# Causal attention with 16 heads of 64: query, key and value projections in three rounded terms instead of whole fp32

## What is computed

```python
def _L3_xattn_ref(q, k, v, Wq, Wk, Wv, Wo):
    query = jnp.einsum('bse,hed->bhsd', q, Wq)
    key_p = jnp.einsum('bse,hed->bhsd', k, Wk)
    value = jnp.einsum('bse,hed->bhsd', v, Wv)
    scores = jnp.einsum('bhqd,bhkd->bhqk', query, key_p) / jnp.sqrt(64)
    causal = jnp.tril(jnp.ones((S, S), dtype=scores.dtype))
    scores = scores + (1.0 - causal) * NEG
    alphas = jax.nn.softmax(scores, axis=-1)
    attention = jnp.einsum('bhqk,bhkd->bhqd', alphas, value)
    attention = attention.reshape(B, S, NUM_HEADS * VALUE_DIM)
    return jnp.einsum('bsf,fe->bse', attention, Wo)
...
x = x + _L3_xattn_ref(_layernorm(x), ctx_1024, ctx_1024, Wq, Wk, Wv, Wo)
```

## Time and profile before

| | us |
|---|---|
| median of 3 runs | 1894.47 |
| lowest, highest | 1890.64, 1900.73 |
| the profiled execution | 1900.78 |
| its span in the trace | 1899.0 |
| TensorE busy | 1516.8 (80%) |
| VectorE busy | 963.4 (51%) |
| stage of the change, from its first transfer to the last score step | about 1371 to 1815 |

### The profile page before, as it was taken

How to read it: one execution, slowest core, us unless ns; L and a number is a source line. 1 busy time by engine, 2 the same in 40 slices (tenths; PEclk the granted TensorE clock), 3 DMA queues, 4 the chain that set the end, 5 groups by cost and what they waited for, 6 DMA issues and landing times. The chain is left out here.

```text
span 1899.0 us, 34141 instructions
## 1 busy us (share of the span) xinstructions
PE 1516.8 (80%) x12506; PEld 1188.3 (63%) x12506; DVE 963.4 (51%) x1962; ACT 688.9 (36%) x1527; POOL 493.3 (26%) x833
## 2 busy tenths in 40 slices
PE   3898684865878842999458999997699999999876
PEld 2565473754656542888336666664378888888765
DVE  2676352446645541111456677776326655555652
ACT  1565333321544410111126656665342323332121
POOL 2210027016534303000411355540032323332110
PEclk8899778886889855999769999998799999999986
DMA  5331192446644226886466645452120000000001
GB/s 137 80 77 39 50 351 80 144 139 155 158 109 107 56 83 244 312 313 221 133 155 135 143 104 115 113 114 47 37 73 7 7 7 2 7 7 2 2 7 45
DMA packets 89772, 195.51 MB, mean 103 GB/s; under 512 B 14000, under 2 KB 62512, under 8 KB 81040
## 3 DMA queue, kind: packets, MB, share of 16 engines
q1 hardware_dynamic: 76688, 172.97, 32.2%
q0 software_dynamic: 4608, 12.59, 2.1%
q10 hardware_dynamic: 8320, 7.87, 1.2%
HBM read 136.37 MB, written 57.02 MB: 102 GB/s over the span
## 5 line engine op out<-in xcount | busy, mean ns | idle before, releaser
L987 DVE TENSOR_REDUCE a_sb_mx<-a_mx 128x4 f32<-128x1024 f32 x192 | 234.7, 1222 | 116.6 <-PE a_mx L809 114.0
L730 ACT ACTIVATE a_sb_probs<-a_ex 128x512 f32<-128x512 f32 x384 | 208.8, 598 | 154.7 <-PE a_ex L830 154.3
L1349 DVE RECIPROCAL a_sb_rden<-a_ot 128x256 f32<-128x256 f32 x64 | 112.0, 1750 | 99.4 <-PE a_ot L1233 99.4
L830 PE MATMUL a_ex<-a_sb_QP,a_sb_KP 49*128 49x256 f32 x768 | 99.5, 336 | 32.6 <-ACT a_sb_probs L730 25.9
L266 POOL DMA_INDIRECT a_sb_landing<-f_y_slots,g_pos x48 | 46.6, 970 | 277.6 <-POOLq L143 264.2
L830 PEld LDWEIGHTS a_ex<-a_sb_QP,a_sb_KP 49*128 49x128 f32 x768 | 61.3, 192 | 87.6 <-issue 57.2
L809 PE MATMUL a_mx<-a_sb_KP,a_sb_QP 48*128 48x256 f32 x768 | 89.5, 310 | 33.1 <-DVE a_sb_mx L987 21.2
L843 PE MATMUL a_ot<-a_sb_probs,a_sb_v 128*32 128x256 f32 x1536 | 109.2, 404 | 2.1 <-ACT a_sb_probs L730 2.1
L809 PEld LDWEIGHTS a_mx<-a_sb_KP,a_sb_QP 48*128 48x128 f32 x768 | 62.9, 197 | 45.6 <-DVE a_sb_mx L987 25.5
L1135 POOL TENSOR_TENSOR a_sb_q_lo<-a_sb_whole,a_sb_q_hi 128x512 fp32r<-128x512 f32 x32 | 40.6, 1269 | 172.6 <-ACT a_sb_q_hi L1164 172.6
L2670 PE MATMUL f_hb<-f_sb_xsT,f_sb_wb 128*128 128x128 f32 x640 | 75.2, 279 | 10.9 <-ACT f_sb_xsT L2623 10.9
(11 more groups left out here) (414 smaller groups left out, 3554.2 us busy)
## 6 DMA issues: line engine op xcount, KB each, us to landing
f_sb_wb<-f_w SPq DMA_DIRECT2D x20, 2052.0 KB, 10.2
a_q_moved<-a_sb_qs SPq DMA_DIRECT2D x24, 512.0 KB, 6.1
a_sb_QP<-a_q_moved SPq DMA_DIRECT2D x48, 256.0 KB, 4.0
a_sb_kvT<-ctxT SPq DMA_DIRECT2D x32, 256.0 KB, 3.4
a_k_moved<-a_sb_ks SPq DMA_DIRECT2D x16, 512.0 KB, 4.2
a_sb_KP<-a_k_moved SPq DMA_DIRECT2D x32, 256.0 KB, 5.6
a_sb_QP<-a_q_moved SPq DMA_DIRECT2D x48, 128.0 KB, 4.5
f_x_slots<-f_sb_zero SPq DMA_DIRECT2D x1, 6144.0 KB, 20.0
```

What stands on the lines that cost most here:

```text
L730: act.activation(probs[:, group % 3, 2 * (u % 2) + par], EX[par][:], ACT.Exp, scale=scale)\
L830: op = pe.matmul(EX[par][:, t, :], KP[at:at + R + 1, b % KB, u % KM, t * P:(t + 1) * P], QP[at:at + R + 1, b % 3, u, :], start=True, stop= ...
L987: dve.tensor_reduce(pair, MX[:], AX.X, ALU.max, negate=True).then_inc(mx_read, 1)
L1349: dve.reciprocal(rden[:, n], OT[n][:, 1, :])
```

## The change

Weights, transposed x and context are each held as two fp32r parts: the value rounded (`_hi`) and what the rounding left (`_lo`). Each fp32 matmul of a projection becomes three fp32r matmuls that add up in PSUM: weights_hi by x_hi, weights_hi by x_lo, weights_lo by x_hi. The three weights are rounded (ACT) and split (DVE) once, at the start. They land from memory in buffers that are filled later: wq and wk in the two halves of `v2`, wv in two thirds of `probs`. For each batch x is now rounded by ACT out of the PSUM bank and the rest is taken by DVE from the same bank, which frees it; the context is rounded by ACT and the rest taken by POOL, in a new unit `kv` ahead of q2. The output projection y stays fp32.

```diff
               ("max4", 1), ("max5", 1), ("neg0", 1), ("y", 2),
-              ("max6", 1), ("max7", 1), ("q2", 0), ("q3", 0), ("k0", 0), ("neg1", 1),
+              ("max6", 1), ("max7", 1), ("kv", 0), ("q2", 0), ("q3", 0), ("k0", 0), ("neg1", 1),
               ("score0", 1), ("score1", 1), ("k1", 0), ("k2", 0),
...
             return sems[-1]
-        wq, wk, wv = (sb(n, [P, KD, H * hd]) for n in ("wq", "wk", "wv"))
+        both = lambda n, s: (sb(f"{n}_hi", s, F32R), sb(f"{n}_lo", s, F32R))
+        wgt = {a: both(f"w{a}", [P, KD, H * hd]) for a in "qkv"}
         wo = sb("wo", [P, C, D])
...
         xn = sb("xn", [P, TT, D])
-        xnT = sb("xnT", [P, KD, S])
-        kvT2 = sb("kvT", [P, 2, KD, S])
+        xnT = both("xnT", [P, KD, S])
+        kv, kvT = sb("kv", [P, 2, KD, S]), both("kvT", [P, KD, S])
         whole = sb("whole", [P, 2, 2, S])
...
 
-        first_in, weights_in = sem("first_in"), sem("weights_in")
+        weights_in = sem("weights_in")
+        w_in, w_rounded, w_split = ({a: sem(f"w{a}_{n}") for a in "qkv"} for n in ("in", "rounded", "split"))
+        x_rounded, kv_rounded, kv_split = sem("x_rounded"), sem("kv_rounded"), sem("kv_split")
         kv_in = [sem(f"kv_in{i}") for i in range(2)]
...
 
-        first_loads = [(wq[:], w["wq"].rearrange("(k p) n -> p k n", p=P)),
-                       (wk[:], w["wk"].rearrange("(k p) n -> p k n", p=P))]
+        landing = {"q": v2[:, 0].rearrange("p t h d -> p (t h d)"), "k": v2[:, 1].rearrange("p t h d -> p (t h d)"),
+                   "v": probs[:, 0:2].rearrange("p n j t s -> p (n j t s)")}
+        w_whole = {a: landing[a].rearrange("p (k n) -> p k n", k=KD) for a in "qkv"}
         halves = [slice(0, P // 2), slice(P // 2, P)]
...
         loads += [(eye[rows, i], io["c_eye"][halves[i]]) for rows in halves for i in range(2)]
-        loads += [(wv[:], w["wv"].rearrange("(k p) n -> p k n", p=P)),
-                  (wo[:], w["wo"].rearrange("(c p) n -> p c n", p=P))]
-        first_all, all_in = 16 * len(first_loads), 16 * len(loads)
+        loads += [(wo[:], w["wo"].rearrange("(c p) n -> p c n", p=P))]
+        all_in = 16 * len(loads)
+        terms = [(0, 0), (0, 1), (1, 0)]
 
...
                 if b >= 2:
-                    done(sp, gp_full, gp, ("v3", b - 2))
-                sp.dma_start(kvT2[:, b % 2], io["ctxT"][b].rearrange("(k p) s -> p k s", p=P)).then_inc(kv_in[b % 2], 16)
-
-            for dst, src in first_loads:
-                sp.dma_start(dst, src).then_inc(first_in, 16)
-            load_context(0)
+                    sp.wait_ge(kv_split, b - 1)
+                sp.dma_start(kv[:, b % 2], io["ctxT"][b].rearrange("(k p) s -> p k s", p=P)).then_inc(kv_in[b % 2], 16)
+
+            for a in "qkv":
+                sp.dma_start(w_whole[a], w[f"w{a}"].rearrange("(k p) n -> p k n", p=P)).then_inc(w_in[a], 16)
+                if a == "q":
+                    load_context(0)
             for dst, src in loads:
...
                     a, i = what[0], number(what) if what[-1].isdigit() else 0
-                    if what in small and a in "qk":
+                    if what == "kv":
+                        pool.wait_ge(kv_rounded, b + 1)
+                        pool.tensor_tensor(kvT[1][:], kv[:, b % 2], kvT[0][:].bitcast(F32), ALU.subtract).then_inc(kv_split, 1)
+                    elif what in small and a in "qk":
                         done(pool, gp_read, gp, (what, b))
...
             norm_sqrt(act, g, sqrt_in, sqrt_out)
+
+            def round_weights(a):
+                act.wait_ge(w_in[a], 16)
+                act.activation(wgt[a][0][:], w_whole[a], ACT.Copy).then_inc(w_rounded[a], 1)
+
+            round_weights("q")
             for step in steps:
...
                         done(act, gp_full, gp, (what, b))
-                        act.activation(xnT[:], GP[bank][:], ACT.Copy).then_inc(gp_read[bank], 1)
+                        act.activation(xnT[0][:], GP[bank][:], ACT.Copy).then_inc(x_rounded, 1)
+                        if b == 0:
+                            round_weights("k")
+                    elif what == "kv":
+                        if b >= 1:
+                            done(act, gp_full, gp, ("v3", b - 1))
+                        act.wait_ge(kv_in[b % 2], 16 * (b // 2 + 1))
+                        act.activation(kvT[0][:], kv[:, b % 2], ACT.Copy).then_inc(kv_rounded, 1)
+                        if b == 0:
+                            round_weights("v")
                     elif what in small and a in "qk":
...
                         k = prr.place[u]
+                        if k == 0:
+                            act.wait_ge(w_split["v"], 1)
                         if k >= 3:
...
         def _(pe):
-            def features(u, wgt, n0, rhs):
+            def features(u, a, n0, rhs):
                 for c in range(2):
-                    for k in range(KD):
-                        op = pe.matmul(GP[gp.slot(u)][:, c, :], wgt[:, k, (n0 + c) * P:(n0 + c + 1) * P], rhs[:, k, :],
-                                       start=(k == 0), stop=(k == KD - 1))
+                    for i, (of_w, of_x) in enumerate(terms):
+                        for k in range(KD):
+                            op = pe.matmul(GP[gp.slot(u)][:, c, :], wgt[a][of_w][:, k, (n0 + c) * P:(n0 + c + 1) * P],
+                                           rhs[of_x][:, k, :], start=(i == 0 and k == 0), stop=(i == 2 and k == KD - 1))
                 op.then_inc(gp_full[gp.slot(u)], 1)
 
-            def tokens(u, lhs, wgt, n0):
+            def tokens(u, lhs, n0):
                 for t in range(TT):
-                    for k in range(KD):
-                        op = pe.matmul(GP[gp.slot(u)][:, t, :], lhs[:, k, t * P:(t + 1) * P], wgt[:, k, n0:n0 + D],
-                                       start=(k == 0), stop=(k == KD - 1))
+                    for i, (of_w, of_x) in enumerate(terms):
+                        for k in range(KD):
+                            op = pe.matmul(GP[gp.slot(u)][:, t, :], lhs[of_x][:, k, t * P:(t + 1) * P],
+                                           wgt["v"][of_w][:, k, n0:n0 + D], start=(i == 0 and k == 0), stop=(i == 2 and k == KD - 1))
                 op.then_inc(gp_full[gp.slot(u)], 1)
...
                         if b == 0 and i == 0:
-                            pe.wait_ge(first_in, first_all)
+                            pe.wait_ge(w_split["q"], 1)
                         if i == 0:
                             done(pe, gp_read, gp, ("xT", b))
-                        features(u, wq, 2 * i, xnT)
+                        features(u, "q", 2 * i, xnT)
                     elif what in small and a == "k":
+                        if b == 0 and i == 0:
+                            pe.wait_ge(w_split["k"], 1)
                         if i == 0:
-                            pe.wait_ge(kv_in[b % 2], 16 * (b // 2 + 1))
-                        features(u, wk, 2 * i, kvT2[:, b % 2])
+                            pe.wait_ge(kv_split, b + 1)
+                        features(u, "k", 2 * i, kvT)
                     elif what in small and a == "v":
                         if b == 0 and i == 0:
-                            pe.wait_ge(weights_in, all_in)
-                        tokens(u, kvT2[:, b % 2], wv, i * D)
+                            pe.wait_ge(w_split["v"], 1)
+                        tokens(u, kvT, i * D)
                     elif what.startswith("max"):
...
                             done(pe, ot_read, otr, (f"weigh{last}", b))
+                        if b == 0:
+                            pe.wait_ge(weights_in, all_in)
                         bank = gp.slot(u)
...
             norm_factors(dve, g, sqrt_in, sqrt_out)
+
+            def split_weights(a):
+                dve.wait_ge(w_rounded[a], 1)
+                dve.tensor_tensor(wgt[a][1][:], w_whole[a], wgt[a][0][:].bitcast(F32), ALU.subtract).then_inc(w_split[a], 1)
+
             dve.memset(negT[:].bitcast(F32), 0.0)
...
                         normalise(dve, g, b, xn, xn_ready)
+                        if b == 0:
+                            split_weights("q")
+                    elif what == "xT":
+                        dve.wait_ge(x_rounded, b + 1)
+                        dve.tensor_tensor(xnT[1][:], GP[bank][:], xnT[0][:].bitcast(F32), ALU.subtract).then_inc(gp_read[bank], 1)
+                        if b == 0:
+                            split_weights("k")
+                            split_weights("v")
                     elif what in small and a == "v":
```

## The result

| | before | after |
|---|---|---|
| median, us (20 runs each) | 1896.62 | 1902.80 |
| lowest, highest | 1889.27, 1900.75 | 1895.75, 1910.62 |
| the profiled execution | 1900.78 | 1910.62 |
| its span | 1899.0 | 1908.8 |

The ratio is 1.003, with a 95% interval of 1.0017 to 1.0044. The time lies in the range that was given and within 0.5% of before, but on the other side of before than the forecast, and by more than its interval.

A forecast was written before the change was run, and what follows sets the result against it. PE's own work was taken to bound the stage. Batch 0 (-1.7), projections (-25.9), VectorE's lag (+16.2) and the clock (+10.2) summed to -1.2 us, giving 1893.3 us, with a range of 1880 to 1904.

The forecast's parts named there:

- what the projections cost and will cost: Projection units on PE: 1.36 us instead of 1.73, 0.37 less each; 25.9 us less over batches 1 to 7.
- Batch 0: Start of the stage, with weights rounded and split: its first eight units end at 1401.6 against 1403.26, 1.7 us less.
- VectorE's lag: Ahead of q0, batches 2 to 7: x's subtraction queues behind weigh6 and weigh7, q0 2.70 us late; 16.2 us more.
- The clock: Behind each of six waits ahead of q0: half clock for 3.4 us, 1.7 us lost each; 10.2 us more.
- The prediction's own bounds for the matmul: Time per fp32r projection record, 0.12 or 0.108 us around the 0.113 taken: the sum becomes +4 or -5 us.
- At nothing: Per batch, ahead of q2: the context's rounding (ACT 0.6) and rest (POOL 1.27) cost nothing; uncovered, 1.9 us ahead of k0.
- The first (the clock holds, 1883, 11.4 less): The clock stays full through the waits ahead of q0: -11.4 us, 1883 us; chance 0.20.
- The second (VectorE isn't late): No lag ahead of q0, so v2 and v3 of batches 1 to 6 gain too: -32.0, 1862.5 us; chance 0.07.
- The third (slower by longer stretches): Behind the six waits the clock stays low longer, 5.1 us lost each: +19.3, 1914 us; chance 0.10.
- The fourth: In the projections, weight loads don't hide behind matmuls on the same rows: +91, 1985 us; chance 0.03.

The follow-up runs named there:

- e2: The changed kernel, with 24 extra fp32r matmuls on PE filling the wait ahead of q0 in six steps; 1893.38 us, 0.9984 of before.
- e4: The changed kernel, with each matmul of q and k made as two of 128 moving columns instead of one of 256; 2034.42 us, one run.
- e3: The kernel before, projections still fp32, with xT's copy out of PSUM made by VectorE instead of ACT; 1924.47 us, 1.0149 of before.
- e6: The changed kernel with xT first, x split by ACT and POOL, and weigh7 moved behind max3; 1873.85 us, 0.9902 of before.
- e1: The changed kernel, with unit xT first in the step instead of behind weigh7; 1893.55 us, 0.9984 of before.
- e5: The changed kernel, with xT first in the step and x split by ACT and POOL instead of VectorE; 1876.59 us, 0.9902 of before.
- e8: The changed kernel, with each matmul of v over 512 moving columns instead of 256 (values not the layer's); 1946.84 us, one run.
- e7: As e6, with the rounding of wv in batch 0 moved behind q0's copies; 1874.77 us, 0.99 of before.

## Why the prediction was wrong, point by point

**Which step failed.** The term "what the projections cost and will cost". The mechanism is right: PE's own work is the step, and it became less by twelve units. The size was wrong: 0.113 us for an fp32r record of 256 columns, taken from the 64 records of the earlier trace rows; measured 0.120, the upper bound that I had from the score matmuls of the earlier trace rows. A unit saves 0.296 (e2) and not 0.37, and 70 units 20.7 us instead of 25.9. The reason given, that array, rows and weight loads are the same in the earlier trace rows, was true and beside the point: at 17 columns (before) as at 128 (e4) such a record takes 0.111, so a pitch of 0.113 could not tell what 256 columns take. Two rows were at hand, and the one with the right number of columns was the right one. The forecast's sum was -1.2, the sum by measured terms is +6.1 (below): of the 7.3 between them this term has 5.2, batch 0 has 1.4, the clock 0.6 and the lag 0.1.

**Batch 0**, the second miss: predicted 1.7 less, measured 0.3 less. The issue to landing, ACT's rounding (1.91 for 1.92 predicted) and VectorE's split (2.29 for 2.2) were right, and q0 started 9.9 us after the first transfer, as worked out. But k0 waited 1.60 us for q2's copies behind wv's rounding, and k2 another 0.66. The second has its cause on POOL, whose two rests of q, begun while VectorE split wv, took 3.78 us, 2.54 for the first and 1.27 for the second; I had POOL at 1.27 each.

**VectorE's lag**: right. 2.70 us predicted; e3, with nothing else changed, has 2.69, and in the changed kernel the way from q2 to the next q0 grew by 42.04 - 41.70 = 0.34 while 8 units saved 2.37: 2.71. The wait itself was predicted as 3.44 and is 3.26, less by what v2 and v3 save less.

**The clock**: right in total, by two misses that cancel. Predicted were six stretches of 3.4 us at half speed, 1.7 lost in each, 10.2. Found were three of 3.4 and three of 6.8, and the way from q0 to q2, which shows the loss, is 13.82 or 14.83 us, against 13.11 - 2 x 0.296 = 12.52 without one: 1.3 and 2.3 lost, 10.8 in all. It is less than half a stretch each, since a part of the stretch lies inside the wait (5.30 of 6.80 us are busy), and an fp32r record goes from 0.120 to 0.213 us at half clock, not to 0.240, so that 44% is lost of each busy microsecond: 0.44 x 5.30 = 2.3 and 0.44 x 3.04 = 1.3.

**The sum by measured terms**: -0.3 - 20.7 + 6 x 2.71 + 10.8 = +6.1, against the stage's 6.6 and the medians' 6.2. The prediction's own bounds for the matmul gave +4 at 0.12; with batch 0 as it was, that would have been nearly the result. With two bounds that put the sum on either side of zero (+4 and -5), which way the time would go hung on the value taken between them. That the time stayed within 0.5% of before, as forecast, is partly luck: a gain that was priced too high stood against losses that were priced nearly right.

**At nothing**: right. No wait of PE ahead of k0 in any batch from 1 on. The rests of the context took POOL 1.3 us a batch, beside PE.

**The rivals.** The first (the clock holds, 1883, 11.4 less) is what e2 makes of the change with PE kept busy: 1893.4, 2.5 less than the before beside it. Its number had the projections' gain 5.2 too high and batch 0's 1.4; the other 2 lie within e2's interval (7 less to 1 more). The second (VectorE isn't late) is what e6 built; the time given for it was 1862.5, and at 0.296 a unit it is about 82 x 0.296 = 24.3 less than before. The stage of e6's profile is 24.2 less, its median 19.1 less. The third (slower by longer stretches) did not occur after all in this kernel, but such stretches exist: in e4 the same wait brings 17.1 us. The fourth fell with the first row of the projections: weight loads of 128 x 128 stand ahead of every record, on the same rows, and a record takes 0.120. The Trainium skill ("TensorE: Matmul & The Clock Gate", Part 3, The mechanism) has the loads overlap only where the row group differs; the trace does not agree with that.

## What to carry to other kernels

When an engine has no idle time and its work is made shorter, ask first who is next in its queue of releasers, and where in that releaser's own queue a new instruction lands: 0.68 us of work put at the wrong end of VectorE's queue cost 2.7 us a step and the clock with it, and given to other engines left a gain of 1%. When an unknown instruction is priced from a nearest row, match the size that sets its time and not only its form; a row of the same form with far fewer columns tells whether columns set it at all (17 columns took as long as 128); and if the sum's sign hangs on the choice, give the bounds as two cases. A short wait on a TensorE that is busy everywhere else can cost more in clock than in waiting (e1: 1.2 us of wait, 1.6 of clock), so a wait is worth removing or filling even where it looks small.

## What the runs showed of the hardware that was not expected

- **Short waits and the clock.** With dense work on both sides, in this stage: behind 0.60 us the granted clock never fell (e5, six of six held); behind 1.19 us it fell in all six (e1); behind 2.33 in four of six (e8) and behind 2.69 in four of six (e3); behind 3.26 in all six (after, and again in e4). The length of the wait alone does not order these, and each is one profiled execution.
- **The same wait, different stretches.** Behind 3.26 us the clock stood at 0.50 for 3.4 or 6.8 us by turns in the changed kernel, and for 17.1 us where the projections had records of 128 columns (e4), though PE was busy in 16.15 of them.
- **A floor under a record with new weights**, fp32 or fp32r: 0.111 us at full clock, with 17 columns (before, fp32) as with 128 (e4, fp32r); 0.213 at half clock with 128 columns (e4). An fp32r record of 256 columns also takes 0.213 at half clock (after), so that columns beyond 128 up to 256 cost nothing there and 0.009 at full clock.
- **POOL beside VectorE.** A subtraction of 128 x 512 on POOL takes 1.26 to 1.28 us. Where VectorE subtracts two tensors of 128 x 2048 in SBUF at the same time, POOL comes almost to a stand: in e7 1.27 us of overlap made it 1.13 us longer, and in batch 0 of after and of e6 1.38 us of overlap made it 2.54 long instead of 1.27. The Trainium skill ("GPSIMD Engine Reference", 1. Specifications) names contention between the two where VectorE has two SBUF inputs; the trace agrees, and shows its size.
